# A vision tower's front end reordered: patch normalisation moved into the weights, block 0 by halves with fp32r products

## What is computed

```python
x = _layernorm(patches, ln1_w)             # over 768 values: (x - mu) * rsqrt(var + EPS) * gamma
x = jnp.einsum('bnd,ed->bne', x, W)        # 768 -> 256
x = _layernorm(x, ln2_w)                   # over 256 values
h = concat(cls_tok, x + pe)                # 37 tokens
# block 0: n = layernorm(h); Q, K = rope(n @ qw), rope(n @ kw); V = n @ vw; causal softmax
h = h + attention(n) @ ow
# experts, top-k over the tokens of each expert
scores = softmax(layernorm(h) @ gate_w.T).T
topk_weight, topk_idx = jax.lax.top_k(scores, 74)
```

## Time and profile before

| | |
|---|---|
| median of 3 runs | 932.23 us (931.94 to 936.35) |
| profiled execution | 932.26 us |
| span of its profile | 930.5 us |
| TensorE busy | 839.1 us (90%) |
| VectorE busy | 661.7 us (71%) |
| ScalarE busy | 458.1 us (49%) |
| GpSimd busy | 253.8 us (27%) |

### The profile page before, as it was taken

The page is one execution under the profiler, slowest core; times in us unless marked ns, Lnnn a source line. Parts: engine busy times, 40 slices in busy tenths (PEclk is TensorE's granted clock), DMA queues, the critical chain, the costliest instruction groups (busy, mean ns, idle before and its releaser), DMA issues.

```text
span 930.5 us, 16226 instructions
## 1 busy us (share of the span) xinstructions
PE 839.1 (90%) x5890; PEld 765.4 (82%) x5890; DVE 661.7 (71%) x1298; ACT 458.1 (49%) x788; POOL 253.8 (27%) x297
## 2 busy tenths in 40 slices
PE   1898689999999999879999998999999999989788
PEld 0676677799999998779898898998988889879556
DVE  6434756848878877477878778787787777875586
ACT  3015323133333333467667676766756766744421
POOL 0000211001111112035435526415524543532232
PEclk9969987999999999889999999999999999997989
DMA  4000019369989981201021011002102102020000
GB/s 166 0 1 1 1 63 369 114 228 311 343 317 317 315 313 37 94 1 35 12 92 34 11 45 52 27 11 90 34 11 90 34 11 90 1 94 1 1 1 27
DMA packets 18289, 88.34 MB, mean 95 GB/s; under 512 B 3120, under 2 KB 7472, under 8 KB 12240
## 3 DMA queue, kind: packets, MB, share of 16 engines
q1 hardware_dynamic: 18256, 87.90, 26.8%
HBM read 85.05 MB, written 2.84 MB: 94 GB/s over the span
## 4 chain that ended last, share of the span: by engine, by line
PE 44%; issue 25%; POOL 17%; DVE 9%; ACT 3%; DMA 1%; SPq 0%; POOLq 0%; DVEq 0%; ACTq 0%
PE bank L992 12%; POOL W_L L1708 6%; PE bank L1029 5%; POOL arena L1686 4%; POOL HF_L L1744 3%; PE bank L763 3%; PE bank L708 3%; PE bank L1135 2%; POOL WQKV_L L1708 2%; PE bank L881 2%; PE bank L1038 2%; PE bank L1309 1%; POOL SQ L1714 1%; PE bank L862 1%; PE bank L717 1%
## 5 line engine op out<-in xcount | busy, mean ns | idle before, releaser
L992 PE MATMUL bank<-arena 128*128 (+1 forms) x1024 | 117.9, 274 | 0.5 <-ACT arena L1442 0.5
L992 PEld LDWEIGHTS bank<-arena 128*128 128x128 f32 x1024 | 117.3, 192 | 0.7 <-ACT arena L1442 0.7
L1686 POOL TENSOR_TENSOR arena<-arena,srec 111x456 f32<-111x456 f32 x56 | 51.8, 953 | 175.1 <-DVE srec L1852 175.1
L763 PE MATMUL bank<-XHL,W_H 128*128 128x296 f32 x384 | 89.7, 312 | 0.0
L763 PE MATMUL bank<-XHL,WQKV_H 128*128 128x296 f32 x288 | 74.0, 331 | 9.0 <-DVE XHL L2188 4.9
L1708 POOL TENSOR_TENSOR W_L<-LW,W_H 128x256 fp32r<-128x256 f32 x96 | 70.1, 768 | 18.9 <-ACT W_H L1502 18.9
L1744 POOL TENSOR_TENSOR HF_L<-arena,HF_H 128x296 fp32r<-128x296 f32 x48 | 43.9, 936 | 114.0 <-ACT HF_H L1603 114.0
L1698 POOL TENSOR_TENSOR QW<-QW,arena x14 | 20.8, 1484 | 180.9 <-DVE arena L2079 110.0
L763 PEld LDWEIGHTS bank<-XHL,W_H 128*128 128x128 f32 x384 | 65.5, 192 | 0.7
L763 PEld LDWEIGHTS bank<-XHL,WQKV_H 128*128 128x128 f32 x288 | 50.0, 196 | 16.1 <-DVE XHL L2188 8.0
L1864 DVE TENSOR_SCALAR OB<-bank,lvec 96x148 f32<-96x148 f32 x144 | 51.2, 368 | 15.6 <-PE bank L833 13.1
(11 more groups left out here) (240 smaller groups left out, 2168.5 us busy)
## 6 DMA issues: line engine op xcount, KB each, us to landing
arena<-ew_in SPq DMA_DIRECT2D x16, 2048.0 KB, 9.1
arena<-ew_in SPq DMA_DIRECT2D x16, 1024.0 KB, 6.8
LW<-lw_in SPq DMA_DIRECT2D x12, 1024.0 KB, 5.0
arena<-route SPq DMA_DIRECT2D x32, 185.0 KB, 3.4
LW<-lw_in SPq DMA_DIRECT2D x6, 768.0 KB, 4.4
fp_weights<-arena SPq DMA_DIRECT2D x1, 2048.0 KB, 6.4
arena<-fp_weights SPq DMA_DIRECT2D x1, 2048.0 KB, 7.3
arena<-patches_in SPq DMA_DIRECT2D x2, 864.0 KB, 6.0
```

What stands on the lines that cost most here:

```text
L763: last = mm(o, w, x, start=(i == 0), stop=(i == len(pairs) - 1))
L992: last = mm(o[:, m * CAP:(m + 1) * CAP], w[:, kc, mi * P:(mi + 1) * P], xg(kc, e), start=(kc == 0), stop=(kc == C - 1))
L1686: nc.gpsimd.tensor_tensor(v, v, srec[0:QROWS, s:s + 2, :].unsqueeze(3).to_broadcast([QROWS, 2, C * JH, KEYS]), ALU.mult).then_inc(p_ready, 1)
```

## The change

- Loads: `Wt` first, then param, both patch halves, const, amask, `w0_16`, and `gate_w` with them.
- `LN_PATCH` is gone. VectorE takes from each row of `Wt` its mean over the 256 outputs and scales it by `ln1_w` (so that the mean over the outputs of a token is zero), TensorE sums the scaled weights over the partitions, VectorE subtracts that mean (so that a token's own mean falls out). The products take the raw patches. What remains of the first normalisation is a factor per token, which the second one removes but for its EPS: `eps_var` carries EPS * (variance of the patch + EPS) as the bias of the second root (`patch_stats`, `token_eps`, `token_root`).
- Sums over chunks are three additions on VectorE (`sum_chunks`) in place of a strided reduction.
- The two halves are staggered on all engines through `LN_TOK`, `LN_ATT0` and the rope and value products.
- Block 0's weights are cast to fp32r (exact for fp16 values), its stream to XH (fp32r) and the rest XL; every output of rope and values is four fp32r products, `block0_products`. Each output has its own place in the ring of six banks; VectorE waits for single outputs (`rope`). The output projection keeps fp32 (`WO0`).
- `gather_values` moves from VectorE to ScalarE (after pairs 3, 5 and 7, and at the end); the projection of half 0 stands before pair 6 (`PROJECT_AT`), and `LN_MOE` of half 0 beside the rest.
- Logits and transposes of U are split by half; the copy of scores into `scoreT` is ScalarE's, two memsets of VectorE come earlier.

```diff
-    for h in range(2):
-        jobs += [("w", 2 * h + c) for c in range(C)] + [("v", 4 * h + i) for i in range(4)]
+    jobs = [("r", i) for i in range(8)] + [("w", 0), ("w", 1)]
+    jobs += [("r", 8 + i) for i in range(4)] + [("v", i) for i in range(4)]
+    jobs += [("r", 12 + i) for i in range(4)] + [("w", 2), ("w", 3)] + [("v", 4 + i) for i in range(4)]
...
+        if p == PROJECT_AT:
+            jobs += [("p", 0), ("p", 1)]
...
@@ TensorE
-            both_ln(LN_PATCH, ones_p, lambda h: pe.wait_ge(patch_sum, h + 1))
+            for kc in range(PC):
+                pe.wait_ge(tok_w_scaled, kc + 1)
+                last = mm(bank[4][:, 0:D], ones_p[:, :], Wt[:, kc, :], start=(kc == 0), stop=(kc == PC - 1))
+            last.then_inc(tok_w_mean, 1)
...
+            tokens(0, 0, 0, PC)
+            tokens(0, 1, 0, PC)
+            patch_stats(0)
+            tokens(1, 0, 0, PC // 2)
+            ln_var_of(LN_TOK, 0, ones_d)
+            tokens(1, 0, PC // 2, PC)
+            pe.wait_ge(ld_const, 32)
+            ln_bcast_of(LN_TOK, 0)
+            patch_stats(1)
+            tokens(1, 1, 0, PC // 2)
+            pe.wait_ge(h_ready, 1)
+            ln_mean_of(LN_ATT0, 0, ones_d)
+            tokens(1, 1, PC // 2, PC)
+            ln_var_of(LN_ATT0, 0, ones_d)
+            ln_var_of(LN_TOK, 1, ones_d)
+            ln_bcast_of(LN_ATT0, 0)
+            ln_bcast_of(LN_TOK, 1)
+
+            def block0_products(key, g, c, h, first):
+                free_bank(0, BLOCK0, key)
+                o = bank_of(BLOCK0, key)[:, 0:NHALF]
+                for part in (XH, XL):
+                    for kc in range(C):
...
+                        last = mm(o, W0R[:, kc, g, c * P:(c + 1) * P], part[:, h, kc, :],
+                                  start=(part is XH and kc == 0), stop=(part is XL and kc == C - 1))
+                last.then_inc(filled[key[0]], 1)
...
+            rope_products(0, 0)
+            pe.wait_ge(h_ready, 2)
+            ln_mean_of(LN_ATT0, 1, ones_d)
+            rope_products(0, 1)
+            value_products(0)
+            ln_var_of(LN_ATT0, 1, ones_d)
+            ln_bcast_of(LN_ATT0, 1)
+            rope_products(1, 0)
+            turn_v(0, BLOCK0, 0)
+            rope_products(1, 1)
+            value_products(1)
+            turn_v(0, BLOCK0, 1)
...
@@ ScalarE
+            block0_high(0)
+            act.wait_ge(cleared, 1)
+            queries_out(0)
+            keys_out(0)
+            ln_square(LN_ATT0, 1)
+            queries_out(1)
+            ln_root(LN_ATT0, 1)
+            keys_out(1)
+            block0_high(1)
             values_out(0, BLOCK0, 0)
+            f(WO0, w0_16[:, :, 5], ACT.Copy)
+            for n in (2, 3):
+                queries_out(n)
+                keys_out(n)
...
+                if p in (3, 5, 7):
+                    gather_values((p - 3) // 2)
+            ln_square(LN_MOE, 0)
+            gather_values(3)
+            ln_root(LN_MOE, 0)
...
+            act.wait_ge(moe_dve, MOE_DVE["scoreT"])
+            f(scoreT[0:E, 0:4 * P], bank[5][0:E, 0:4 * P], ACT.Copy)
+            mark(f(scoreT[0:E, 4 * P:N], bank[6][0:E, 0:N - 4 * P], ACT.Copy), "scoreT")
...
@@ VectorE
+            link(v.tensor_reduce(wsum[:, :], Wt, AX.X, ALU.add))
+            link(v.tensor_scalar(wsum[:, :], wsum[:, :], 1.0 / D, None, ALU.mult))
+            for kc in range(PC):
+                v.tensor_scalar(Wt[:, kc, :], Wt[:, kc, :], wsum[:, kc:kc + 1], prm("ln1_w", kc),
+                                ALU.subtract, ALU.mult).then_inc(tok_w_scaled, 1)
+            dve.wait_ge(tok_w_mean, 1)
+            for kc in range(0, PC, 2):
+                v.tensor_tensor(Wt[:, kc:kc + 2, :], Wt[:, kc:kc + 2, :], over_chunks(bank[4][:, 0:D], 2), ALU.subtract
+                                ).then_inc(tok_w_ready, 1)
...
             for h in range(2):
                 dve.wait_ge(ld_patch if h == 0 else ld_patch2, 16)
-                patch_chunks(h, patches[:, :, h, :], 0)
+                sum_chunks(h, patches[:, :, h, :], CNp, 0)
+                dve.wait_ge(patch_squared, h + 1)
+                sum_chunks(h, SQp[:, h, :, :], SQp, 1)
...
+            token_eps(0)
+            ln_recip(LN_TOK, 0)
+            token_rows(0)
+            token_eps(1)
+            dve.wait_ge(h_ready, 1)
+            ln_centre(LN_ATT0, 0)
+            ln_recip(LN_ATT0, 0)
+            ln_recip(LN_TOK, 1)
+            block0_scale(0)
             v.memset(Ke[:, :, :, :, :, T:KEYS], 0.0)
             clear_value_pads()
+            block0_low(0)
+            token_rows(1)
             dve.wait_ge(cleared, 1)
...
+            rope(0, 0)
+            dve.wait_ge(h_ready, 2)
+            ln_centre(LN_ATT0, 1)
+            rope(0, 1)
+            ln_recip(LN_ATT0, 1)
+            block0_scale(1)
+            block0_low(1)
+            rope(1, 0)
             spread_values(0, BLOCK0, 0)
+            rope(1, 1)
             spread_values(0, BLOCK0, 1)
...
-            v.tensor_copy(scoreT[0:E, 0:4 * P], bank[5][0:E, 0:4 * P])
-            v.tensor_copy(scoreT[0:E, 4 * P:N], bank[6][0:E, 0:N - 4 * P])
             v.tensor_copy(work[0:E, 0:4 * P], bank[5][0:E, 0:4 * P])
-            v.memset(work[0:E, N:N + 8], -1.0)
-            v.memset(ones_n[0:E, :], 1.0)
             mark(v.tensor_copy(work[0:E, 4 * P:N], bank[6][0:E, 0:N - 4 * P]), "scoreT")
```

More of the change, by code:

```diff
@@ new lines, in _, with tokens @@
+            last.then_inc(tok_w_mean, 1)
+            def tokens(h, c, lo, hi):
+                o = bank[2 * h + c]
+                for kc in range(lo, hi):
+                    if (h, c) == (0, 0) and kc % 2 == 0:
+                        pe.wait_ge(tok_w_ready, kc // 2 + 1)
+                    if (c, kc) == (0, 0):
+                        pe.wait_ge(ld_patch if h == 0 else ld_patch2, 16)
+                    last = mm(o[:, 0:NP_HALF], Wt[:, kc, c * P:(c + 1) * P], patches[:, kc, h, :],
+                              start=(kc == 0), stop=(kc == PC - 1))
+                if hi == PC:
+                    last.then_inc(tok_psum, 1)
@@ L2429, in counts @@
     return out
[L2432 to L2433 removed]
+MOE_PE = counts(["ut0", "ut1", "logits", "ut2", "ut3", "ut4", "scoreT", "posT", "shared"] + [f"xg{i}" for i in range(8)])
+MOE_ACT = counts(["ut0", "ut1", "exp", "ut2", "ut3", "ut4", "scoreT"] + [f"xg{i}" for i in range(8)])
 MOE_DVE = counts(["shift", "probs", "scoreT", "pos", "onehot0", "onehot1", "onehot2", "onehot3"])
```

386 lines of the change are left out of this document (220 added, 166 removed).

## The result

The changed kernel takes 902.77 us (median of 4 runs, 901.4 to 906.43) where the kernel before takes 932.29 in the same comparison; the ratio is 0.968, with a 95% interval of 0.9645 to 0.9714. Forecast were 904 us, 892 to 918. Its profiled execution took 901.4 us around a span of 899.6.

What follows compares the result with a forecast made beforehand. Latencies between engines were taken to bound the kernel up to the first HS product: stages 38.2 + 29.6 + 38.5 + 12.7 + 5.0 = 124.0 against 154.2, less 1.8 for gaps, gave -28.4 and 903.9 us; range 892 to 918.

Steps and rivals of the forecast that it cites:

- The bound: Up to the first HS product latencies between engines set the time; it ends 28.4 us sooner, all behind moves along.
- Stage A: Start to first rope product: 65.5 us before, 38.2 forecast, a gain of 27.3.
- rival (4): Folded weights wait for the DMA or fp32r misses 0.137; each costs about 1 to 4 us, within the forecast's range.
- Stage B: First rope product to first scores: 32.7 us before, 29.6 forecast, a gain of 3.1.
- Little of it counts: Stage B: fp32r outputs save TensorE 9 us, but VectorE and ScalarE set the pace, so little is gained.
- Stage C: First scores to last projection: 36.1 us before, 38.5 forecast, a loss of 2.4, with gathers queued on ScalarE.
- Stages D and E: D, last projection to scoreT: 15.6 us to 12.7; E, on to the first HS product: 4.4 to 5.0.
- E's mechanism: ScalarE copies scores before UT_H, table load and gelu; VectorE's first product waits for that gelu, idling some 2 us.
- The same within 1 us: From the first HS product to the end the time stays equal within 1 us, otherwise the prediction is wrong.
- Half clock to the gates: TensorE's clock stays at half from rope products to gates: about 935 us, no change; chance 0.03 (slower: 0.02).
- ScalarE as the bound: Slow gathers and queues on ScalarE lengthen stages B and C by 8 to 15 us: about 915 us; chance 0.24.
- A change that doesn't do what it says: The same as rival (4): weights wait for the DMA, or fp32r is slower; about 1 to 4 us each.

Runs made afterwards that it cites:

- Wt late: Changed kernel, but SP issues the load of Wt after patches, const and amask, just before block 0's weights; 911.75 us.
- changed, again: The changed kernel run and profiled once more with no edit; 903.81 us.
- fp32 products: Changed kernel, but each rope and value output of block 0 is two fp32 products again instead of four fp32r; 909.51 us.
- both of these: Changed kernel with block 0's rope and value products back in fp32 and VectorE waiting for four outputs again; 912.72 us.

## Why the prediction was right, and where it was not

**The bound.** Right: up to the first HS product latencies between engines set the time, and all behind moves with it. 28.4 us were predicted for that point, 28.4 were measured (154.19 to 125.81). That the two agree to the tenth is luck: the second profile of the same kernel has its first HS product at 129.59, which is 24.6.

**Stage A.** Right, and by its own steps: first patch product forecast at 14.5, measured 14.35; VectorE's sums to 23.7 and 23.31; the first rope product at 38.2 and 37.45. The weights were there by 5.56 (6.0 forecast); what VectorE waited for was param (to 5.26), queued behind Wt. The row sum over 1536 contiguous values took 1.75 us (1.7 forecast, though its own terms give 1.8), where the strided one took 3.06 for 1728. That the load order carries part of the gain was underrated: 6.2 us, by "Wt late", where rival (4) had put 1 to 4 for weights that wait. How the rest of A's 28 us divides between the folded norm and the halves was not tried.

**Stage B.** The size was right (29.6 forecast, 29.4 measured), the reason wrong. The step that failed is "Little of it counts" of the fp32r products, with the gain given to the ring. The runs show 4.2 us for the products alone, 2.6 for VectorE's single waits alone, 7.7 for both, and, argued and not tried, 4.4 lost to the second half's norm. What the places in a ring of six banks are worth by themselves was not tried either. I compared TensorE's pace with VectorE's and ScalarE's in the steady part and did not count that the products stand ahead of the next norm in TensorE's own queue, though my walk had that norm's broadcast behind the values. fp32r ran at 0.152 in the dense stretch, not 0.137. ScalarE did not release most waits, as I had put it: of the idle time that the trace lists in B, 6.7 us ended on ScalarE, 9.5 on VectorE and 8.3 on TensorE.

**Stage C.** A loss was forecast, 2.4 us, and it was 4.3. "here the change does not pay" is right, but the cause named, the gathers on ScalarE, is not: back on VectorE they change 0.1 us of the stage, and up to the last variance they were a gain of 1.6. The cause is the order at the end of the stage, the first half's broadcast ahead of the second half's projection, with ScalarE's table load (1.28 us) on its way; swapping them gives all of it back (36.02). The step that failed is that C's account has the gathers and half 0's projection in the middle, and no wait of the second projection behind that broadcast.

**Stages D and E.** 12.7 and 5.0 forecast, 13.5 and 5.1 measured, D above the 11 to 13 that I had set as its sign, and 16.0 in the second profile, at half clock. E's mechanism holds as put: VectorE idled 2.05 us in front of its first product, released by the gelu, and moving the copies gives 1.1 to 1.9 us back:

```profile
124.83 0.42 ACT L1601 ACTIVATE XD<-bank 128x296 f32<-128x296 f32 x1
...
125.35 0.46 DVE L2249 TENSOR_TENSOR LW<-XD,bank 128x296 f32<-128x296 f32 x1 [2.05 <-ACT XD L1601]
```

**From there to the end.** "The same within 1 us" was wrong for the pair of profiles: 773.8 us against 776.3, and I had written that such a difference makes the prediction wrong. It is right for the work: through the layers the two stay apart by 27.5 to 27.6 us, and the last layer's one stretch of 35.0 or 37.8 us makes the difference: 2.8, with 0.8 lost ahead of the layers and 0.6 won behind that stretch. That a second profile of the same kernel has 36.1 there shows that a part of it comes with the execution; that all of the 2.8 does is likely, not shown. Ahead of the layers the kernels differ too: from the end of the first HS product to 425 us the kernel before takes 0.8 us less than the changed kernel, "changed, again" 0.3 more, fp32 products and "both of these" 2.1 and 2.4 more.

**The rivals.** Half clock to the gates: no, though the clock fell at or just behind each of the three places where the prediction had put sparse stretches (0.58 from 38 to 42, 0.58 from 47 to 55, 0.63 from 64.3 to 68), and rose again each time (1.00 from 42 to 47 and from 55 to 64). The mean of B was 0.80, before 0.89. That is the direction of the rule that small idle times between groups of products, as they cycle through PSUM banks, let the clock fall again and again (the Trainium skill, TensorE: Matmul & The Clock Gate, "A second HAM failure mode: psum-queue depth-cycling"). But the ring alone does not bring it here: with the same ring and fp32 products, which keep TensorE busy 30.1 us of 33.6 instead of 23.5 of 29.6, the mean is 0.91. With VectorE waiting for four outputs it is 0.82. No run takes the ring away. ScalarE as the bound: no; it was busy 18.1 us of B's 29.6 and three times waited for VectorE there, 7.2 us in all, in front of its spreads of queries. A change that doesn't do what it says: no.

## What to carry to other kernels

When the halves of a batch are staggered over engines that work in order, look on each queue for a product that needs nothing being put behind one that waits for a root or a table: swapping two such lines was worth 4.4 us of its stage here, as much as the change of precision in its own (4.2); by the medians the swap gave 3.6 us and the precision 6.5. A faster product can count even where its pace does not meet the bound, if it stands ahead of the next chain's first step. And before a difference of 1 to 3 us in a stage or behind the changed part is explained, profile the same kernel twice.

## What was not expected of the hardware

- The same instructions of the last layer took 35.0, 36.1 or 37.8 us, nothing between, in 14 profiles, and in the three profiles shown above the clock fell in other places: over one piece in the middle, 3.2, 3.3 and 4.6 us long, its mean was 0.84, 0.75 and 0.50. From 425 to 803 us of the changed kernel all profiles kept their distance from one another within some 0.1 us.
- In one execution TensorE stayed at half clock from 108.4 to 124.5 us although it was busy 14.2 of these 16.1 us, mostly with products of 1, 16 and 128 columns; in another the same stage had a mean of 0.72.
- ScalarE's strided copies of 148 columns out of PSUM took 0.28 us each, VectorE's 0.37.
- With filler products of 2.1 and 1.3 us in front of sparse stretches the clock was 1.00 from 63.5 to 77.2 us in one kernel; in another, with the same filler, it was 0.77 from 61.7 to 64 and 0.76 from 64 to 69, then 1.00. Each is a single profile, so how much of the first is the filler's doing is open.
